# Routing tokens to experts by a table of slots: one-hot matmuls build it, tiles gather their rows and scatter their results

## The reference, cut to what matters

```
x = x + tanh(g_xattn[0]) * depool(layernorm(x), ctx_2048)        # a decay scan over 1601 rows, gathered per token
x = x + tanh(g_ffn[0])   * switch_ffn(layernorm(x))              # top 1 of 8 experts
x = x + tanh(g_xattn[1]) * attention(layernorm(x), ctx_2048)     # 8 heads, 1601 keys, masked
x = x + tanh(g_ffn[1])   * moe_ffn(layernorm(x))                 # top 2 of 8 experts

switch_ffn:  e = argmax(x @ router_w + b);  y = (silu(a) * g) @ w2[e] with a, g = split(x @ w1[e]);  y * max_prob
moe_ffn:     e1, e2 = top2(silu(x @ rw1 + rb1) @ rw2 + rb2);  p = softmax of the two logits
             y = sum over both of p_e * (silu(x @ w1[e] + b1[e]) @ w2[e] + b2[e])
```

## Time and profile before

| | us |
|---|---|
| median of 3 runs | 1506.59 |
| lowest and highest of them | 1505.58, 1506.63 |
| the profiled execution | 1506.97 |
| its span, first to last instruction | 1505.2 |
| PE busy, share of the span | 1194.0, 79% |
| DVE, ACT, POOL busy | 517.4, 464.9, 426.9 |
| DMA: mean rate over the span | 140 GB/s |

### The profile page before, as it was taken

How to read it: one execution, slowest core, us unless ns; L and a number is a source line. 1 busy time by engine, 2 the same in 40 slices (tenths; PEclk the granted TensorE clock), 3 DMA queues, 4 the chain that set the end, 5 groups by cost and what they waited for, 6 DMA issues and landing times.

```text
span 1505.2 us, 19220 instructions
## 1 busy us (share of the span) xinstructions
PE 1194.0 (79%) x6998; PEld 842.6 (56%) x6998; DVE 517.4 (34%) x1249; ACT 464.9 (31%) x1067; POOL 426.9 (28%) x467
## 2 busy tenths in 40 slices
PE   2455299999976789999999999688803999999960
PEld 2245299999973444454454453222202898888850
DVE  1474122221116776676676672100140000000013
ACT  1211022221100345655555556312201333333310
POOL 1050300000015265575575666400043000000025
PEclk9975599999996799999999999899956999999985
DMA  9310577888851000000000000000015999999954
GB/s 310 129 56 0 210 289 285 295 302 304 316 185 45 1 1 2 0 1 1 1 1 1 1 1 1 0 1 0 0 58 198 323 332 323 331 328 336 324 191 129
DMA packets 61083, 211.24 MB, mean 140 GB/s; under 512 B 9787, under 2 KB 40125, under 8 KB 44349
## 3 DMA queue, kind: packets, MB, share of 16 engines
q1 hardware_dynamic: 50912, 183.22, 34.6%
q0 software_dynamic: 5376, 14.69, 3.1%
q10 hardware_dynamic: 4700, 12.10, 2.2%
HBM read 183.64 MB, written 26.35 MB: 140 GB/s over the span
## 4 chain that ended last, share of the span: by engine, by line
PE 71%; DVE 9%; POOL 6%; issue 5%; DMA 4%; ACT 3%; SPq 1%; ACTq 1%; POOLq 0%; DVEq 0%
PE PQ L371 20%; PE PB L385 14%; PE PB L476 7%; PE PQ L461 6%; PE PQ L526 4%; PE PB L445 4%; PE PB L267 4%; PE PB L466 3%; DVE Z L809 3%; PE PQ L445 2%; PE PB L505 2%; POOL xs L1150 2%; DVE SM L546 1%; POOL Z L1160 1%; POOL SM L1058 1%
## 5 line engine op out<-in xcount | busy, mean ns | idle before, releaser
L371 PE MATMUL PQ<-Z,WS 128*128 128x128 f32 x2720 | 329.5, 278 | 18.2 <-DMA WS<-in_w 9.9
L371 PEld LDWEIGHTS PQ<-Z,WS 128*128 128x128 f32 x2720 | 324.0, 194 | 31.1 <-issue 26.6
L385 PE MATMUL PB<-WS,Z 128*128 128x256 f32 x992 | 234.3, 379 | 0.0
L809 DVE TENSOR_REDUCE Z<-PB 128x1 f32<-128x402 f32 x340 | 183.5, 567 | 87.4 <-PE PB L445 86.0
L385 PEld LDWEIGHTS PB<-WS,Z 128*128 128x128 f32 x992 | 179.1, 190 | 19.3
L461 PE MATMUL PQ<-QS,KS 128*128 128x512 f32 x416 | 173.3, 438 | 7.3 <-ACT Z L1015 4.5
L953 ACT ACTIVATE Z<-PQ,WS 128x128 f32<-128x128 f32 x312 | 88.9, 368 | 198.6 <-PE PQ L371 198.6
L445 PE MATMUL PB<-KS,QS 128*128 128x402 f32 x340 | 132.8, 401 | 17.3 <-DVE Z L809 9.0
L1015 ACT ACTIVATE Z<-PQ 128x512 f32<-128x512 f32 x208 | 109.7, 604 | 87.2 <-PE PQ L461 87.0
L461 PEld LDWEIGHTS PQ<-QS,KS 128*128 128x128 f32 x416 | 77.2, 191 | 104.5 <-issue 55.3
L1015 ACT ACTIVATE WS<-PQ 128x512 f32<-128x512 f32 x208 | 109.3, 605 | 79.4 <-PE PQ L461 79.3
(11 more groups left out here) (222 smaller groups left out, 1220.4 us busy)
## 6 DMA issues: line engine op xcount, KB each, us to landing
WS<-in_w SPq DMA_DIRECT2D x62, 1024.0 KB, 6.7
WS<-in_w SPq DMA_DIRECT2D x23, 2048.0 KB, 7.9
WS<-in_w SPq DMA_DIRECT2D x39, 1028.0 KB, 7.3
Z<-xs SPq DMA_DIRECT2D x62, 128.0 KB, 7.5
ys<-Z SPq DMA_DIRECT2D x62, 128.0 KB, 6.0
xs<-WS ACTq DMA_DIRECT2D x6, 1024.0 KB, 9.9
Z<-in_b SPq DMA_DIRECT2D x39, 128.0 KB, 7.0
X<-in_x SPq DMA_DIRECT2D x4, 512.0 KB, 10.4
```

What stands on the lines that cost most here:

```text
L371: t = e.matmul(bank[:, j * P:j * P + P], w[:, k, o:o + P], FXT[i % 2][:, k * P:k * P + P], start=k == 0, stop=k == 1)
L385: t = e.matmul(y, FS[c % 4][:, j * P:j * P + P], w[:, 4 * n + j, :], start=n == 0 and j == 0, stop=n == 1 and j == 3)
L809: e.tensor_reduce(MP[j % 2][:, i:i + 1], PB[bank_of["pc", r]][:, 0:PIECE], AX.X, ALU.max).then_inc(v_pc, 1)
```

## The change

Tokens are no longer moved to sorted scratch. Each normed chunk is stored plainly, by SP, in DRAM scratch xn0 or xn1, behind 128 rows of zeros (two DMAs of 128 KB by ACT take the place of the eight). DVE splits each position into tile and lane, builds one-hot matrices, and PE multiplies them (16 matmuls in layer 0, 32 in layer 1) into a table `tabi` that says for every tile and lane which row it holds, and `tabp` with its weight. POOL gathers an x tile by the table (`fetch`) and scatters a result tile by the same column (`give`): in layer 0 into scratch yd, which SP loads back in four DMAs of 512 KB, in layer 1 straight onto the output with an add in the DMA, after SP has stored X there behind attention. Tiles 0 to 7 are those of experts 0 to 7 by construction, so their weights load without a register; the rest fill tiles 8 on. SP's loads no longer wait for the routing, except for those into WS[1], where the one-hot matrices lie. DVE multiplies each result tile with `tabp`, in layer 1 in an instruction behind the bias. The code that makes the table, the loop on POOL and SP's new order:

```diff
@@ PE, behind ranks(l)
+            def tables(l):
+                nt, cc = (NT0, NT1)[l], NC * (1 + l)
+                lanes, _, vals = slot_table(l)
+                for q in range(cc):
+                    if q % 8 == 0:
+                        e.wait_ge(v_slot[l], q // 8 + 1)
+                    t = e.matmul(PB[6][:, 0:2 * nt], lanes[:, q, :], vals[:, q, :, :].rearrange("p s t -> p (s t)"),
+                                 start=q == 0, stop=q == cc - 1)
+                t.then_inc(t_tab[l], 1)
...
@@ route, DVE
-                vc.step(e, e.tensor_scalar(bas, bas, float(P), None, ALU.mult))
+                vc.step(e, e.tensor_scalar(bas, bas, float(P), float(7 * P), ALU.mult, ALU.add))
+                vc.step(e, e.scalar_tensor_tensor(far, CT[:, C_IO8:C_IO8 + E], float(P), bas, ALU.mult, ALU.subtract))
...
+                vc.step(e, e.scalar_tensor_tensor(i3, r3, float(P), far.unsqueeze(2).broadcast_to([P, E, cc]), ALU.is_lt,
+                                                  ALU.mult))
                 vc.step(e, e.tensor_tensor(r3, r3, bas.unsqueeze(2).broadcast_to([P, E, cc]), ALU.add))
+                vc.step(e, e.tensor_tensor(rk[:, 0:n], rk[:, 0:n], inc[:, 0:n], ALU.add))
                 vc.step(e, e.tensor_tensor(rk[:, 0:n], rk[:, 0:n], OH[:, 0:n], ALU.mult))
                 vc.step(e, e.tensor_reduce(pos[:, 0:cc], rk[:, 0:n].rearrange("p (e c) -> p c e", e=E), AX.X, ALU.add))
-                e.tensor_copy(posi[:, 0:cc], pos[:, 0:cc]).then_inc(v_pos[l], 1)
...
+                vc.step(e, e.tensor_copy(posi[:, 0:cc], pos[:, 0:cc]))
+                vc.step(e, e.tensor_single_scalar(posi[:, 0:cc], posi[:, 0:cc], 7, ALU.arith_shift_right))
+                vc.step(e, e.tensor_copy(tile[:, 0:cc], posi[:, 0:cc]))
+                vc.step(e, e.scalar_tensor_tensor(lane[:, 0:cc], tile[:, 0:cc], -float(P), pos[:, 0:cc], ALU.mult, ALU.add))
+                lanes, hot, vals = slot_table(l)
+                vc.step(e, e.tensor_tensor(hot, CT[:, C_IOT:C_IOT + nt].unsqueeze(1).broadcast_to([P, cc, nt]),
+                                           tile[:, 0:cc].unsqueeze(2).broadcast_to([P, cc, nt]), ALU.is_equal))
+                for k in range(picks):
+                    vc.step(e, e.tensor_tensor(row[:, k * NC:(k + 1) * NC], CT[:, C_TP:C_TP + NC],
+                                               lane[:, k * NC:(k + 1) * NC], ALU.subtract))
+                e.scalar_tensor_tensor(vals[:, :, 0, :], row[:, 0:cc].unsqueeze(2).broadcast_to([P, cc, nt]),
+                                       float(P - 1), hot, ALU.add, ALU.mult)
+                e.tensor_tensor(vals[:, :, 1, :], hot, pr[:, 0:cc].unsqueeze(2).broadcast_to([P, cc, nt]), ALU.mult)
+                for q in range(0, cc, 8):
+                    e.tensor_tensor(lanes[:, q:q + 8, :], iota128.unsqueeze(1).broadcast_to([P, 8, P]),
+                                    lane[:, q:q + 8].unsqueeze(2).broadcast_to([P, 8, P]), ALU.is_equal).then_inc(v_slot[l], 1)
...
+                e.wait_ge(t_tab[l], 1)
+                e.tensor_scalar(tabi[:, 0:nt], PB[6][:, 0:nt], CT[:, C_TP:C_TP + 1], -1.0, ALU.add,
+                                ALU.add).then_inc(v_tab[l], 1)
+                e.tensor_copy(tabp[:, 0:nt], PB[6][:, nt:2 * nt]).then_inc(v_tab[l], 1)
@@ experts, DVE
-                        e.tensor_copy(FY[i % 2], y).then_inc(v_y[l], 1)
+                        e.tensor_scalar(FY[i % 2], y, tabp[:, i:i + 1], None, ALU.mult).then_inc(v_y[l], 1)
...
-                        e.tensor_tensor(FY[i % 2], y, FB[i % 2], ALU.add).then_inc(v_y[l], 1)
+                        vc.step(e, e.tensor_tensor(FY[i % 2], y, FB[i % 2], ALU.add))
+                        e.tensor_scalar(FY[i % 2], FY[i % 2], tabp[:, i:i + 1], None, ALU.mult).then_inc(v_y[l], 1)
@@ start, ACT
-            for i, buf, nt in ((0, xs0, NT0), (1, xs1, NT1)):
...
+            for l, buf in ((0, xn0), (1, xn1)):
+                e.dma_start(buf[0:P, :], zero).then_inc(d_zero[l], 16)
@@ experts, POOL
+            def experts(l, nt, xn, into, **add):
+                def fetch(i):
+                    if i >= 2:
+                        e.wait_ge(t_tr[l], bank_of["xt", l, i - 2])
+                    e.indirect_dma_start(FXL[i % 2], None, xn, bass.IndirectOffsetOnAxis(
+                        ap=tabi[:, i:i + 1].bitcast(U32), axis=0)).then_inc(d_xl[l][i % 2], 16)
+
+                def give(i):
+                    e.wait_ge(v_y[l], i + 1)
+                    if i:
+                        e.wait_ge(d_y[l][(i - 1) % 2], landed(i - 1, 2))
+                    e.indirect_dma_start(into, bass.IndirectOffsetOnAxis(ap=tabi[:, i:i + 1].bitcast(U32), axis=0),
+                                         FY[i % 2], None, **add).then_inc(d_y[l][i % 2], 16)
+
+                e.wait_ge(v_tab[l], 2)
...
+                fetch(0)
+                fetch(1)
+                for i in range(nt):
+                    if i + 2 < nt:
+                        fetch(i + 2)
+                    give(i)
+
+            experts(0, NT0, xn0, yd)
...
-            fetched(0)
             power(rst[:, 0:4], 5)
-            queries(0)
-            queries(1)
-            for g in range(1, 4):
-                fetched(g)
-            for j in range(2, 6):
+            for j in range(6):
                 queries(j)
...
+            experts(1, NT1, xn1, out, compute_op=ALU.add)
@@ SP
+            for c in range(NC):
+                e.wait_ge(v_xn, c + 1)
+                e.dma_start(xn0[(c + 1) * P:(c + 2) * P, :], XN[c % 4]).then_inc(d_xn[0][c % 4], 16)
+            def free0(i):
+                if i == 1:
+                    e.wait_ge(t_tab[0], 1)
...
+            experts(0, NT0, w01, w02, free0)
...
+            for g in range(4):
+                e.dma_start(WS[1][:, 2048 + 1024 * g:3072 + 1024 * g].rearrange("p (c d) -> p c d", d=D),
+                            yd[P + 512 * g:P + 512 * g + 512, :].rearrange("(c p) d -> p c d", p=P)).then_inc(d_yd[g], 16)
...
+            for g in range(4):
+                e.wait_ge(v_x3, 2 * g + 2)
+                e.dma_start(out[P + 512 * g:P + 512 * g + 512, :].rearrange("(c p) d -> p c d", p=P),
+                            X[:, 4 * g:4 * g + 4, :]).then_inc(d_res, 16)
```

More of the change, by code:

```diff
@@ L124, in build @@
         m1, m2, pr, tt, pos = sm(NC), sm(NC), sm(2 * NC), sm(NC), sm(2 * NC)
-        cnt, nti, bi, bas = sm(E), sm(E), sm(E), sm(E)
-        mxx, sc7 = sm(80), sm(280)
+        nti, bi, bas, far = sm(E), sm(E), sm(E), sm(E)
+        tile, lane, tabp, row = sm(2 * NC), sm(2 * NC), sm(40), sm(2 * NC)
+        mxx, sc7 = sm(40), sm(280)
+        VW = V.rearrange("p c d -> p (c d)")
         plugi, posi, eidi, ntii, mski = SI[:, 0:16], SI[:, 16:48], SI[:, 48:88], SI[:, 88:96], SI[:, 96:109]
+        tabi = SI[:, 128:168]
         leni, poi, poh = SI[:, 109:122], SI[:, 56:69], SI[:, 69:82]
@@ L177, in build @@
         d_y = [[sem(f"d_y{l}{i}") for i in range(2)] for l in range(2)]
-        d_gr = [[sem(f"d_gr{l}{i}") for i in range((NC, 8)[l])] for l in range(2)]
-        d_rw1, d_out = sem("d_rw1"), sem("d_out")
+        d_yd = [sem(f"d_yd{g}") for g in range(4)]
+        d_rw1, d_res = sem("d_rw1"), sem("d_res")
         v_pad, p_set, a_tg = sem("v_pad"), sem("p_set"), sem("a_tg")
@@ L1183, in _, with experts, row @@
                 e.dma_start(dep_d[c * P:(c + 1) * P, :], DR[c % 2]).then_inc(d_dep[c % 2], 16)
-            def experts(l, nt, xs, ys, w_up, w_down):
+            def experts(l, nt, w_up, w_down, free):
                 up_n = 4 * FF if l == 0 else 2 * FF + 8
                 regs = {}
+                def row(i, n):
+                    return bass.ds(regs[i] * n, n) if i >= E else slice(i * n, i * n + n)
                 def load_up(i):
@@ L1233, in _ @@
-            e.wait_ge(d_clear[0], 48)
-            e.wait_ge(d_clear[1], 80)
-            experts(0, NT0, xs0, ys0, w01, w02)
+                    elif i + 1 < nt:
+                        load_down(i + 1)
+            for c in range(NC):
[4 more added lines that the diff above has]
+                    e.wait_ge(t_tab[0], 1)
+                    for k in range(4):
+                        e.wait_ge(d_xn[0][k], landed(NC - 1, 4))
@@ new lines, in _, with stored, free1 @@
+            e.wait_ge(t_v, 640)
+            def stored():
+                for c in range(NC):
+                    e.wait_ge(v_xr, c + 1)
+                    e.dma_start(xn1[(c + 1) * P:(c + 2) * P, :], XR[c % 4]).then_inc(d_xn[1][c % 4], 16)
+            def free1(i):
+                if i == 1:
+                    stored()
+                    e.wait_ge(t_tab[1], 1)
+            experts(1, NT1, w11, w12, free1)
+            e.wait_ge(d_res, 64)
+            for i in range(2):
+                e.wait_ge(d_y[1][i], landed(NT1 - 1 - (NT1 - 1 - i) % 2, 2))
```

152 lines of the change are left out of this document (48 added, 104 removed).

## The result

The changed kernel takes 1531.94 us (median of 4 runs, 1530.91 to 1540.58), the one before 1506.32 beside it: ratio 1.018, 95% interval 1.015 to 1.022. The forecast was 1477, faster; it came out 25.6 us slower than the kernel before. That is inside the range given for 8 in 10 (1426 to 1549) and outside the forecast's own (1434 to 1504). The profiled execution took 1532.87, its span is 1530.6 against 1505.2.

A forecast was written before the change was run, and what follows sets the result against it. PE was taken to bound the kernel (71% of the chain of waits). 87.5 us won outside the expert loops and 58 lost in layer 1's gave -29.5 us, from 1506.6 to 1477 us; range 1434 to 1504, 8 in 10 1426 to 1549.

The forecast's parts named there:

- 87.5 us: Outside the expert loops: start 7.5, layer 0's routing 14, before attention 5, layer 1's routing 19, end 42 us won.
- room of 9 us: Layer 0's experts: 9.0 us of room a round against 2.5 plus landing, hiding gather landings up to 6.5 us.
- 0.96 (give's issue): Layer 1, POOL: issuing a result tile's scatter takes 0.96 us ahead of the next gather.
- chain of 2.43 us: Layer 1, from result to next gather: bias 0.42, weight 0.45, wake 0.3, scatter issue 0.96, gap 0.3 us.
- 4.5: Layer 1: a gather lands 4.5 us after issue, making rounds 9.17 us and losing 58 us over 36 tiles.
- rival E: Layer 1's experts: PE's stalls bring the clock to 0.5, rounds up to 14 us, 1667 us; chance 0.02.
- the forecast's formula: Layer 1's experts: a round takes 4.67 + L us, L being the gather's landing from its issue.
- Rival B: Layer 1: same stall, larger, deciding from landing 5.3 us; 1549 us at 6.5, 1575 at 7.2; chance 0.21.
- A: Layer 1: gathers land as if queues were idle, up to 3.3 us; 1419 to 1434 us; chance 0.14.
- D: Routing: the change does not shorten it, 33 us less won, about 1510 us; chance 0.04.
- C: Layer 1: the adding scatter is slow and sets the round; landing 12 us gives 1590 us; chance 0.05.
- still hidden, barely: Layer 1: the adding scatter's 5% more bytes, DMA share 0.98 instead of 0.93, stay hidden even without longer rounds.

The follow-up runs named there:

- experiment 6: The kernel before the change with only its clearing DMAs moved behind ACT's squares: 1509.67 us against 1510.29, ratio 0.999.
- 8: The changed kernel with a memset on POOL ahead of each of layer 1's 36 fetches behind a scatter: 1636.41 us, ratio 1.084 to the kernel before.
- 2, plain scatter: The changed kernel with layer 1's scatter overwriting instead of adding: 1499.14 us.
- 3, thin weights: The changed kernel loading only an eighth of layer 1's weight bytes: 1456.74 us.
- 1: The changed kernel with POOL issuing fetch(i + 3) ahead of give(i) in both layers: 1432.13 us, ratio 0.950 to the kernel before.
- 10: The changed kernel with PE and ACT turning layer 1's next tile half a round later: 1455.63 us, ratio 0.965 to the kernel before.
- 9: 4 with four buffers for layer 1's gathered rows, asked for four tiles ahead, and four for its results: 1426.37 us, ratio 0.945.
- 4: 1 with WS[1]'s first weights held back until each layer's first two gathers have landed: 1425.31 us, ratio 0.946 to the kernel before.
- 5: 4 with layer 1's scatter overwriting instead of adding: 1409.86 us, ratio 0.936 to the kernel before.

## Why the prediction was wrong

**Outside the loops it was right.** 87.5 us were forecast, 86.4 came. Within that, table passes were cheaper (0.22 us, not 0.275) and the first gathers dearer, and for the start the cause was another in part (experiment 6). At the end the last scatter landed after 3.9 us, within bounds, but 7.1 us follow its landing where 4.8 were taken over from the last store.

**Layer 0 was right.** From first up matmul to last result it is 261.5 us against 262.6: the room of 9 us hides its gathers, which land after 3.8 us in the median and 5.4 at most.

**Layer 1: the mechanism was right, the size was not.** The step that failed is the term "0.96 (give's issue)" in the chain of 2.43 us, together with "4.5" for the landing. The row for 0.96 was of a scatter that does not add; the one that adds takes 1.59. The row for the landing was of a gather beside one load; the median is 4.9. A third term stood at nothing: behind some stops the eight down passes on the cycle run at the lower clock, which rival E had only for the whole round. With c = 16 x (mean of a down pass - 0.379 us), the forecast's formula becomes 4.67 + 0.63 + L + c for 36 of the 38 rounds, two staying at 7.6. (Passes overlap, so c is rough: from the busy time in the same rows it is 0.41 in the changed kernel and 1.3 in 8, and the two transposes, longer as well, add 0.09 and 0.25, which gives the same sums.)

| kernel | L | added or taken | c | formula, mean of 38 | measured |
|---|---|---|---|---|---|
| changed | 4.9 | 0 | 0.48 | 10.5 | 10.51 |
| 2, plain scatter | 4.5 | -0.60 | 0.38 | 9.5 | 9.58 |
| 3, thin weights | 3.4 | 0 | 0 | 8.6 | 8.51 |
| 8, delay | 5.9 | +0.93 | 1.57 | 13.4 | 13.33 |

The formula meets all four kernels within 0.13 us (measured is from first to last result, by 38), with L and c taken from each trace and not foretold. That the cycle is the cause is shown by the runs that break it (1, 10) or lengthen it (8). Of the 2.96 us by which a round grew against 7.55, the forecast had 1.62; the issue brings 0.63, the landing 0.4, the clock 0.48, each for 36 of the 38 rounds: 3.0 in all.

**The break-even moved with it.** (The prediction's 1504 belongs to an L of 5.2; at 5.3 its own formula gives 1506.) Rival B was to decide from L = 5.3. With 1.59 in the chain it is 4.7, before any clock, and 4.9 lies beyond: the landing came out inside the 3.3 to 5.3 of the forecast, the time outside its 1434 to 1504. The place of the loss, a stop of PE at the gather, once a tile, was the forecast's; the sign turned on 0.6 us that no row of the kernel before had, and without them (experiment 2) the kernel takes 1499.14 us, below the one before.

**The rivals.** A fell (L is 4.9), D fell, and C did not happen in the changed kernel, since rounds of 10.5 us are longer than a scatter; it appears where the rounds are short (1, 9, 10). The sentence that adding costs 5% more bytes, "still hidden, barely", was wrong in those versions: with it 4 is 15 us behind 5. The Trainium skill ("DMA: Bandwidth & Descriptors", "Queues, rings and completion order") states that an engine goes round its queues packet by packet. From that I had reasoned that POOL's gather does not wait for the backlog of SP's weights. L in the loop, 3.5 to 7.5, and 6.2 for the first gather right behind fresh weights against 2.9 without them (experiment 4) do not bear out that a gather is nearly free of it; no run shows the turns themselves.

## What to carry to other kernels

When a transfer moves from one queue's prefetch into another engine's stream, write down the cycle from result to next input before pricing anything: what is on it counts once a round, and issue time, landing and clock all lie there. In an engine's stream put the requests for the next inputs ahead of the handing over of results; here that order was worth 7% of the whole kernel. And an operation that the trace doesn't show (a scatter that adds) deserves an upper bound in every place where it appears, its issue as well as its landing.

## What was unexpected of the hardware

An indirect scatter with an add holds POOL for 1.59 us, the same one without for 0.99, and with the add POOL's queue, gathers included, takes twice the packets. After the 5.15 us stop shown the next 0.7 + 3.6 us of PE's work ran at the lower clock, while after the 2.1 us stop it did not. The length of the stop alone doesn't decide: in the changed kernel eight down passes took 2.85 us behind a stop of 2.46 us and 1.89 behind one of 2.49, and in 8 they took 1.89 behind one of 3.87. In 8 the slower passes and later landings together made 2.8 us a round out of a delay of 0.93. And a gather that goes out 0.6 us or more ahead of a 1 MB load on SP's queue landed after 4.8 us in the median (changed kernel), one that goes out closer to it or behind it after some 6 to 7 (four there, 33 in 8), in 8 with less busy DMA engines; that the load is the cause is likely and untested.
